# Expert products in three passes: high and low parts written by the first stage's norm, effective weights split as they are made, one buffer for output weights

## The reference, cut to what matters

```
# 1: gradient series + gated feed-forward     x = norm(x + ffn(x) + series(x))
# 2: experts (weights from reference setup: W_org 512x512, 8 pairs of lora_down 512x64
#    and lora_up 64x512, keys, Wq)
q      = mean over tokens of x @ Wq.T
coeff  = softmax(q . keys / sqrt(128))            # 8 numbers for all tokens
w_eff  = W_org.T + sum_e coeff[e] * lora_down[e] @ lora_up[e]
x      = norm(x + x @ w_eff)                       # the expert products
# 3: attention over a single key, which is one product with merged weights
w_val  = sum_g wv[g] @ (sum over 4 heads of wo[g]) # g = 0..7
x      = norm(x + x @ w_val)
# 4: quantised gated feed-forward, and so on
```

## Time and profile before

| what | us |
|---|---|
| three timed executions | 1298.91, 1307.59, 1310.77 |
| their median | 1307.59 |
| the profiled execution, its own time | 1303.14 |
| span of its trace, first to last instruction | 1301.4 |
| PE busy, DVE busy, ACT busy | 1228.7, 719.8, 439.8 |
| DMA queue q1 | 78.32 MB, 16.6% of 16 engines |

### The profile page before, as it was taken

One profiled execution on the slowest core, in us unless ns is written; L12 is line 12 of the kernel. 1 busy time (PEld: TensorE's weight loads), 2 busy tenths in 40 slices (PEclk: granted clock), 3 DMA queues, 4 the chain that ended last, 5 costly groups with the idle time before them and its releaser, 6 DMA issues. The chain is left out here.

```text
span 1301.4 us, 14425 instructions
## 1 busy us (share of the span) xinstructions
PE 1228.7 (94%) x5396; PEld 846.3 (65%) x5396; DVE 719.8 (55%) x1194; ACT 439.8 (34%) x751; POOL 162.2 (12%) x215
## 2 busy tenths in 40 slices
PE   7899999998998999998889999999999988999998
PEld 4788688644876788876565445455455534788886
DVE  4422565576657656453355678677767734443344
ACT  2121422212211114222333223666565566222221
POOL 0000000000086201002112110011011224000000
PEclk9999999999999999998999999999999998999999
DMA  8110023423045561004000010000000001022001
GB/s 346 33 49 16 33 97 131 169 97 146 1 146 194 206 229 26 22 1 138 1 1 1 5 44 1 2 2 1 2 2 2 3 2 49 25 73 73 1 25 41
DMA packets 18265, 79.07 MB, mean 61 GB/s; under 512 B 3104, under 2 KB 3872, under 8 KB 16032
## 3 DMA queue, kind: packets, MB, share of 16 engines
q1 hardware_dynamic: 18208, 78.32, 16.6%
HBM read 75.95 MB, written 2.10 MB: 60 GB/s over the span
## 5 line engine op out<-in xcount | busy, mean ns | idle before, releaser
L2427 DVE TENSOR_REDUCE mqa_top<-psum 128x1 f32<-128x512 f32 (+3 forms) x304 | 186.4, 656 | 50.6 <-PE psum L2219 25.0
L2334 ACT ACTIVATE mqa_prob<-psum 128x512 f32<-128x512 f32 x288 | 156.9, 603 | 85.2 <-PE psum L2249 81.2
L612 PE MATMUL psum<-L_ffn_x,L_ffn_w_up 128*128 128x512 f32 x624 | 143.8, 391 | 8.7 <-DVE L_ffn_hidden L767 7.7
L612 PEld LDWEIGHTS psum<-L_ffn_x,L_ffn_w_up 128*128 128x128 f32 x624 | 116.5, 188 | 36.0 <-DVE L_ffn_hidden L767 10.2
L612 PE MATMUL psum<-L_attn_x,L_attn_w_up 128*128 128x512 f32 x456 | 105.4, 393 | 3.9 <-DVE L_attn_hidden L767 3.9
L612 PEld LDWEIGHTS psum<-L_attn_x,L_attn_w_up 128*128 128x128 f32 x456 | 86.6, 190 | 22.5 <-issue 4.3
L2249 PE MATMUL psum<-mqa_stack_back,mqa_keys 100*128 100x512 f32 x208 | 96.3, 463 | 0.9 <-DVE mqa_stack_front L2418 0.9
L2262 PE MATMUL psum<-mqa_prob,mqa_v 128*32 128x512 f32 x576 | 78.8, 614 | 0.0
L2156 POOL TENSOR_SCALAR_AFFINE_SELECT mqa_prob<-mqa_prob 128x512 f32<-128x512 f32 x64 | 41.7, 671 | 256.6 <-ACT mqa_prob L2334 256.3
L2249 PEld LDWEIGHTS psum<-mqa_stack_back,mqa_keys 100*128 100x128 f32 x208 | 40.0, 192 | 49.6 <-ACT mqa_prob L2334 42.8
L2219 PE MATMUL psum<-mqa_keys,mqa_stack_back 96*128 96x512 f32 (+1 forms) x160 | 67.2, 442 | 4.0 <-ACT mqa_stack_back L2327 1.5
(11 more groups left out here) (301 smaller groups left out, 2060.0 us busy)
## 6 DMA issues: line engine op xcount, KB each, us to landing
L_ffn_stage<-in_L_w SPq DMA_DIRECT2D x25, 768.0 KB, 4.6
L_ffn_z_int<-in_L_z SPq DMA_DIRECT2D x14, 768.0 KB, 4.2
L_ffn_s_all<-in_L_s SPq DMA_DIRECT2D x14, 768.0 KB, 6.0
heads_wo<-in_L_wo SPq DMA_DIRECT2D x8, 1024.0 KB, 4.8
L_attn_stage<-in_L_w SPq DMA_DIRECT2D x10, 512.0 KB, 3.7
L_attn_w_down<-in_L_down SPq DMA_DIRECT2D x1, 2560.0 KB, 24.1
x_feat<-in_x_feat SPq DMA_DIRECT2D x2, 1024.0 KB, 7.0
x_tok<-in_x_tok SPq DMA_DIRECT2D x1, 2048.0 KB, 18.6
```

Source lines behind the costliest of these rows:

```text
L612: ins = nc.tensor.matmul(bank[place][:, :], w_up[:, slot, w_part, at:at + P], x_half[half][:, x_part, k, :], start=k == 0 and n == 0, stop ...
L2334: nc.scalar.activation(prob[:, n % PROBS, :], score_bank[n % 3], ACT.Exp, scale=SCALE)\
L2427: nc.vector.tensor_reduce(top[:, i % 2, 2 if lo == qt * P else lo // HALF, heads[0]:heads[-1] + 1], max_bank[n % 3][:, 0:len(heads) * widt ...
```

## The change

- A class `EntryParts` places low parts of the eight entry tiles in free memory (three under the next front, four from byte 139680, where the second `wo` buffer was, one behind), and `x_high`, a float32r name for the memory of `x_feat`, holds the high parts.
- The first stage's tail gets these parts as its `start`: ACT's copies write the high part, and DVE has one more `dve_low` per tile (tiles 0 to 6 in the first stage's loop, tile 7 in the next block ahead of `c.rot.dve`). The transposes of tile t now wait for the low part of tile t-2 instead of ACT's copy.
- `add_tokens` reads the turn bank in PSUM in place of `x_feat`.
- `MergedHeads.SLOTS` goes from 2 to 1: the load of `wo` g is issued when the sum of g-1 is made.
- `w_values` becomes `w_parts` and serves both stages. After each add of `w_eff` DVE waits for ACT's high copy and subtracts it into the low part, before the next add. PE waits for the four low parts (`eff_low`).
- The expert products go in three passes by the same function as the value products; `product_tiles` stays in use elsewhere.
- The delta product i = 3 waits for the low part of entry tile 7. Steps 10 to 12 stand ahead of the expert products and 13 to 19 behind. `add_heads` 7 moves from tile 2 to tile 4.

The diff, cut to its core (arguments that are only passed through are left out):

```diff
@@ -38,6 +38,8 @@
         self.x_tok = self.sb("x_tok", [P, NT, DIM], F32)
+        with ExitStack() as other_name:
+            self.x_high = self.sb("x_high", [P, KC, TOK], F32R, other_name)
         self.x_feat = self.sb("x_feat", [P, KC, TOK], F32)
@@ -377,6 +379,25 @@
+class EntryParts:
+
+
+    def __init__(self, c, at):
+        with ExitStack() as own:
+            c.sb("entry_below_low", [P, at // 4], F32, own)
+            early = c.sb("entry_low_early", [P, 4, KC, P], F32R, own)
+            c.sb("entry_over_low", [P, 4 * KC * DIM // 2], F32, own)
+            late = c.sb("entry_low_late", [P, KC, P], F32R, own)
+            c.sb("entry_over_late", [P, 8192 // 4 - KC * P], F32, own)
+            first = c.sb("entry_low_first", [P, 3, KC, P], F32R, own)
+        self.high = c.x_high
+        self.low = [first[:, t, :, :] for t in range(3)] + [early[:, t, :, :] for t in range(4)] + [late[:, :, :]]
+        self.x_low = c.sem("entry_x_low")
+
+    def x_part(self, part, t):
+        return self.low[t] if part else self.high[:, :, t * P:(t + 1) * P]
+
+
 class FfnStart:
@@ -476,7 +497,7 @@
         g_bank, u_bank = c.bank[0:2], c.bank[2:4]
-        tail = Tail(c, c.bank[4:6], c.bank[6:8], last is not None)
+        tail = Tail(c, c.bank[4:6], c.bank[6:8], last is not None, start=parts)
@@ -816,11 +837,13 @@
                             expert.add_tokens(dve, tail, earlier)
+                            tail.dve_low(dve, earlier)
                     tail.dve(dve, t)
...
                         expert.add_tokens(dve, tail, t - 2)
+                        tail.dve_low(dve, t - 2)
                     if t + 2 < NT:
@@ -1039,12 +1062,13 @@
         dve.wait_ge(tail.feat_ready, tail.base + t + 1)
-        c.nc.vector.tensor_reduce(c.token_sum[:, :, t], c.x_feat[:, :, t * P:(t + 1) * P], AX.X, ALU.add)
+        turned = tail.tr_bank[t % 2].rearrange("p (k n) -> p k n", k=KC)
+        c.nc.vector.tensor_reduce(c.token_sum[:, :, t], turned, AX.X, ALU.add)
...
-    KV, SLOTS, STEPS = 8, 2, 8 * KC
+    KV, SLOTS, STEPS = 8, 1, 8 * KC
@@ -1052,6 +1076,7 @@
             self.wo = c.sb("heads_wo", [P, self.SLOTS, 4, DIM], F32, own)
+            c.sb("heads_below_wv", [P, 4 * DIM], F32, own)
             self.wv = c.sb("heads_wv", [P, self.KV, DIM], F32, own)
@@ -1121,11 +1146,12 @@
         sb("below_values", [P, 2 * TOK + 4 * KC * P // 2 + 2 * DIM - 256 - KC * DIM])
-        w_values, w_eff = c.sb("lora_w_values", [P, 2, KC, DIM], F32R, own), sb("w_eff", [P, KC, DIM])
+        w_parts, w_eff = c.sb("lora_w_parts", [P, 2, KC, DIM], F32R, own), sb("w_eff", [P, KC, DIM])
         parts = Parts(c, start)
...
         tail_values = Tail(c, c.bank[4:6], c.bank[6:8], start=start)
-        values_ready, values_high = sem("values_ready"), sem("values_high")
+        values_ready, values_high, eff_high = sem("values_ready"), sem("values_high"), sem("eff_high")
+        eff_low = sem("eff_low")
         w_loaded, org_loaded, q_loaded = entry.w_loaded, sem("org_loaded"), entry.q_loaded
@@ -1152,6 +1178,18 @@
             def _(pe):
+                def products(into, x, t):
+
+                    if t >= 2:
+                        pe.wait_ge(into.out_taken, into.base + t - 1)
+                    pe.wait_ge(x.x_low, t + 1)
+                    for k in range(KC):
+                        for n, (x_part, w_part) in enumerate(PASSES):
+                            ins = nc.tensor.matmul(into.out_bank[t % 2], x.x_part(x_part, t)[:, k, :],
+                                                   w_parts[:, w_part, k, :],
+                                                   start=k == 0 and n == 0, stop=k == KC - 1 and n == len(PASSES) - 1)
+                    ins.then_inc(into.out_ready, 1)
+
                 x_last = c.x_tok[:, NT - 1, :]
@@ -1174,7 +1212,7 @@
                     if i == KC - 1:
-                        pe.wait_ge(entry.tail.feat_ready, entry.tail.base + NT)
+                        pe.wait_ge(entry_parts.x_low, NT)
                     for r in range(RC):
@@ -1184,28 +1222,20 @@
                     ins.then_inc(delta_ready, 1)
-                heads.products(pe, range(10, 12))
-                pe.wait_ge(eff_ready, KC)
+                heads.products(pe, range(10, 13))
+                pe.wait_ge(eff_low, KC)
                 for t in range(NT):
-                    product_tiles(c, pe, tail, w_eff, t)
+                    products(tail, entry_parts, t)
                     if t:
...
-                heads.products(pe, range(12, 20))
+                heads.products(pe, range(13, 20))
                 tail.pe(pe, NT - 1)
...
                         pe.wait_ge(values_ready, KC)
-                    if t >= 2:
-                        pe.wait_ge(tail_values.out_taken, tail_values.base + t - 1)
-                    pe.wait_ge(parts.x_low, t + 1)
-                    for k in range(KC):
-                        for n, (x_part, w_part) in enumerate(PASSES):
-                            ins = nc.tensor.matmul(tail_values.out_bank[t % 2], start.x_part(x_part, t)[:, k, :],
-                                                   w_values[:, w_part, k, :],
-                                                   start=k == 0 and n == 0, stop=k == KC - 1 and n == len(PASSES) - 1)
-                    ins.then_inc(tail_values.out_ready, 1)
+                    products(tail_values, parts, t)
                     if t:
@@ -1226,13 +1256,16 @@
                 c.rot.act(act)
+                for i in range(KC):
+                    act.wait_ge(eff_ready, i + 1)
+                    nc.scalar.copy(w_parts[:, 0, i, :], w_eff[:, i, :]).then_inc(eff_high, 1)
                 tail.act(act)
...
                     act.wait_ge(heads.merged, i + 1)
-                    nc.scalar.copy(w_values[:, 0, i, :], c.bank[i]).then_inc(values_high, 1)
+                    nc.scalar.copy(w_parts[:, 0, i, :], c.bank[i]).then_inc(values_high, 1)
                 for t in range(NT):
@@ -1276,18 +1309,22 @@
+                entry.tail.dve_low(dve, NT - 1)
                 c.rot.dve(dve)
...
                         .then_inc(eff_ready, 1)
+                    dve.wait_ge(eff_high, i + 1)
+                    nc.vector.tensor_tensor(w_parts[:, 1, i, :], w_eff[:, i, :], w_parts[:, 0, i, :].bitcast(F32),
+                                            ALU.subtract).then_inc(eff_low, 1)
                 for t in range(NT):
...
                         tail.dve_low(dve, t - 1)
-                    if t in (0, 2):
-                        heads.add_heads(dve, 6 + t // 2)
+                    if t in (0, 4):
+                        heads.add_heads(dve, 6 + t // 4)
                     if start is not None and t == 5:
@@ -1297,7 +1334,7 @@
                     dve.wait_ge(values_high, i + 1)
-                    nc.vector.tensor_tensor(w_values[:, 1, i, :], c.bank[i], w_values[:, 0, i, :].bitcast(F32),
+                    nc.vector.tensor_tensor(w_parts[:, 1, i, :], c.bank[i], w_parts[:, 0, i, :].bitcast(F32),
                                             ALU.subtract).then_inc(values_ready, 1)
@@ -2497,14 +2534,15 @@
         heads = MergedHeads(c, 131488)
-        gradient_ffn(c, a, entry, heads)
+        entry_parts = EntryParts(c, 139680)
+        gradient_ffn(c, a, entry, heads, entry_parts)
         c.rot = Rotation(c)
...
             c.sb("below_lora", [P, 4 * front1.width], F32, scope)
-            lora_then_single_key(c, a, front1, start1, entry, heads)
+            lora_then_single_key(c, a, front1, start1, entry, heads, entry_parts)
         swiglu(c, front1, table=c.rot, ahead=conv_weights, a=a, start=start1)
```

More of the change, by code:

```diff
@@ L444, in swiglu @@
            extra_dve=None, extra_pe=None, extra_act=None, extra_split=None, table=None, ahead=None, a=None,
-           start=None, expert=None, heads=None):
+           start=None, expert=None, heads=None, parts=None):
     nc = c.nc
@@ L890, in products, with gradient_ffn @@
         ins.then_inc(self.used, 1)
-def gradient_ffn(c, a, entry, heads):
+def gradient_ffn(c, a, entry, heads, entry_parts):
     nc = c.nc
@@ L1091, in products, with lora_then_single_key @@
                 ins.then_inc(self.merged, 1)
-def lora_then_single_key(c, a, front, start, entry, heads):
+def lora_then_single_key(c, a, front, start, entry, heads, entry_parts):
     nc = c.nc
```

2 lines of the change are left out of this document (1 added, 1 removed).

## The result

The changed kernel takes 1308.81 us (median of 20 executions, 1302.06 to 1314.39), the kernel before in the same comparison 1305.48 (20 executions, 1296.99 to 1310.77). The ratio is 1.0046 with a 95% interval of 1.0027 to 1.0064: slower by some 6 us, by 3.5 at the least, so within 1%. The forecast was 1312.1. The profiled execution of the kernel after took 1312.02 us, that of before 1303.14.

The account below looks back on a forecast made before the run. The prediction took DVE to pace the expert products, with PE waiting for it, and PE to be the path behind. Its terms, 6.46 - 0.54 - 0.34 - 0.86 + 2.0 = 6.7 us, on 1305.4 gave 1312.1 us, range 1302 to 1321.

Parts of the forecast that it names:

- part 4: From tile 0's add to tile 7's transposes: 5.92 us late, less 0.34 and 0.86, so PE 4.7 us late, nothing recovered behind.
- What bounds the kernel: In the expert products DVE sets the pace once tile 0's product is there, and PE waits; behind them PE is the path.
- Part 1: Expert products: three passes save PE 4.5 us, but only 0.54 and 0.34 reach DVE, 0.9 us at the end.
- Part 2: Entry tile 7's low part ahead of the rotation chain: chain and first `w_eff` add 1.8 us later, bounds 1.3 and 1.9.
- Part 3: Split of `w_eff`: serial rounds of 2.09 us, first expert product 6.46 us later, PE waiting 5.4 (3.4 to 6.2).
- Part 5: Low clock behind PE's wait ahead of the expert products: 2.0 us lost, bounds 0 and 2.8.
- Part 6: First-stage low parts, token sum read from PSUM, and loads with one `wo` buffer: all covered, costed at nothing.
- Rival (a): Same PE wait ahead of the expert products, but clock at full: +4.7 us, 1310.1; chance 0.18.
- (b): Loads behind the single `wo` buffer land late and DVE stands at `dequantise`: 5 us on top, 1317; chance 0.10.
- (c): Split hides behind heads' steps, shorter products carry through: 4.5 us off, 1300.9; gain if PE waits under 1.7; chance 0.07.
- (d): Three passes no faster on the expert products' operands: the 0.9 us returns, 1313; chance 0.03.

Follow-up runs that it names:

- heads_ahead: Changed kernel with six more steps of heads ahead of the expert products and fewer behind: 1309.36 us, ratio 1.0045.
- steps_in_stretch: Changed kernel with seven steps of heads moved into PE's waits inside the expert products: 1308.14 us, ratio 1.0050.
- plain_products: Changed kernel with the expert products as plain float32 of the entry's high part and `w_eff`, splits and waits kept: 1304.90 us, ratio 1.0038.
- low_part_in_chain: Changed kernel with entry tile 7's low part inside the rotation chain, where DVE waits for ACT's root, instead of ahead of it: 1310.28 us, ratio 1.0062.
- split_in_a_row: Changed kernel with DVE's four adds of `w_eff` in a row and the four subtractions behind them: 1306.01 us, ratio 1.0017.
- turns_on_pool: Changed kernel with the nine levels of turn factors computed by GpSimd instead of in DVE's chain: 1300.35 us, ratio 0.9981.
- best_with_plain_products: filled_turns_on_pool with plain float32 expert products of the entry's high part and `w_eff`, low part left out: 1298.86 us, ratio 0.9995.
- filled_turns_on_pool: filled plus turn factors on GpSimd, heads sum 6 ahead of the `w_eff` split, next front's second low part behind the value-weight split: 1294.95 us, ratio 0.9943.
- filled: Changed kernel with `w_eff` subtractions one add behind, entry tile 7's low part inside the chain, heads steps inside the stretch: 1303.04 us, ratio 0.9992.
- 14 memsets: Changed kernel with fourteen more GpSimd memsets in the setup, starting everything some 3.4 us later: 1314.86 us, ratio 1.0087.

## Why the prediction was right

It said slower by 6.7 us; the ratio gives 6.0 (3.5 to 8.4), and the two medians of 20 differ by 3.3. The level that it took for the kernel before, 1305.4, is the median of the 20 executions, 1305.48, and that is luck: in the three later comparisons the same kernel stood at 1301.6 to 1302.4. The mechanism is the forecast one, a wait of PE for a split that DVE reaches late. But the size is closer than the sum deserves: in the profile the first value product is 7.8 us later, with one term of the sum wrong by 1.7 us (part 4), and others that partly make up for it. Step by step:

- **What bounds the kernel.** Held. DVE paced the stretch: from tile 0's add to tile 6's no idle time, 26.15 us (26.56 before). It is 26.16 in heads_ahead and 26.15 in steps_in_stretch, whatever PE does there, and 27.20 in plain_products, where the longer products behind tile 0's cost DVE 1.05.
- **Part 1** (0.54 and 0.34 us): -0.41 us in place of -0.34 inside the stretch. The 0.54 shows where the clock is up: 3.10 us from start to add in low_part_in_chain, against 3.64 before.
- **Part 2** (1.8 us): the first add of `w_eff` stands 0.27 us ahead of the first heads row in place of 1.97, so 1.7 later. Taking it away gave 1.46.
- **Part 3** (a round 2.09, PE 6.46 late after a wait of 5.4): 1.98, 6.06 and 5.03. Of the three hand-overs that I had put at 0.04 each, the two between DVE and ACT are 0.03 (264.03 - 264.00, 264.68 - 264.65), and the next add starts 0.08 before the subtraction's row ends. split_in_a_row and turns_on_pool show that this wait comes from the place of the rounds in DVE's order.
- **Part 4** (PE 4.7 us late at the transposes of tile 7): this is the mis-sized term. I gave 0.86 us back for fourteen rows instead of sixteen; between tile 6's add and the first value product 0.84 us were lost instead. The difference, 1.7 us, is the second low clock. Its root stands in part 1, "the rest only lets PE wait longer for DVE", which I costed at nothing. PE's waits for DVE inside the stretch grew from 2.2 to 6.1 us in total, and the clock fell behind the last one. That they are the cause is shown by plain_products and steps_in_stretch, both with shorter waits and no second fall. All thirteen profiles agree: the seven kernels with 6.0 to 6.1 us of these waits have the low clock behind the stretch, and the six with 2.9 us or less have none (before has 2.2). Whether the sum of the waits counts or the longest of them (3.3 us against 2.7 at the most) is not told apart.
- **Part 5** (2.0 us of clock at the head): tile 0's add came 4.97 us after the product's start, 3.10 at full clock: 1.87.
- **Part 6** (nothing): held. The first stage's low part is done before the transposes, which wait no longer than before (6 rounds alike):

```profile
195.73 0.69 DVE L1066 TENSOR_REDUCE token_sum<-psum 128x4 f32<-128x512 f32 x1
...
196.33 0.68 DVE L133 TENSOR_TENSOR entry_low_first<-psum,x_high 128x512 fp32r<-128x512 f32 x1
...
197.83 0.60 PE L155 MATMUL psum<-ident,x_tok 128*128 128x128 f32 x4
```

The sum read from PSUM takes 0.69 us against 0.68. And the loads stand behind tile 0 and its sum of g = 6 at 281, as said, with `dequantise` 18 us later and no wait in brackets:

```profile
280.95 0.33 SPq L1090 DMA_DIRECT2D heads_wo<-in_L_wo  x1
281.32 0.43 SPq L229 DMA_DIRECT2D L_ffn_stage<-in_L_w  x1
...
298.94 1.75 DVE L352 TENSOR_TENSOR L_ffn_stage<-L_ffn_stage,L_ffn_z_int 128x1536 f32<-128x1536 int32 x1
```

- **Rival (a)**, the clock at full: not in the profile, where both lows are seen. **(b)**, late loads: no. **(c)**, the products carry through: not here; with PE's gaps filled they do, for 4.7 us, where it named 4.5. The break-even that (c) names, a wait of 1.7 us, is too high. It leaves out the extra step of heads in front: in turns_on_pool, with no wait, the first expert product starts 0.61 us later than before. And it leaves out the second low clock, by which the first value product is 1.64 us later there. **(d)**, three passes no faster: no, as part 1 shows.

The profile moved by 7.8 us at the first value product, and the time by 6.0, with an interval of 3.5 to 8.4 that holds both. The executions differ in their mean granted clock, and at a like clock the kernels stand nearly in the order of the profiles. At 0.989 to 0.990: before 1298.8 (8 executions of the later comparisons), after 1302.3 (3), plain_products 1304.2 (6), split_in_a_row 1299.5 (4), turns_on_pool 1298.7 (4), best_with_plain_products 1298.0 (6), filled_turns_on_pool 1292.4 (4). This leaves the change 3.4 us. At 0.987 to 0.988 it is 4.7 (before 1302.1, 27 executions; after 1306.8, 7), and at 0.980 it is 3.8 (1308.5, 3; 1312.2, 6). (The executions of the changed kernel are from the first comparison.) All three are near the 4.7 of the sum without its clock term. But this picks executions by a number that the change itself moves, so I read it as a hint.

For low_part_in_chain, steps_in_stretch and filled the first value product is 3 to 11 us earlier than in the changed kernel, and the ratios of the first two show none of it. For steps_in_stretch and filled a part of it (2.6 and 2.4 us) is given back at the low clock of the value products, and that is seen in the profiles: filling PE's gaps made the next wait longer, and the clock fell behind that one. The remainder lies further on. No execution of low_part_in_chain or filled was above a mean clock of 0.985, and none of steps_in_stretch above 0.983, while the kernel before reaches 0.993. Why the later code gets less clock in these kernels is not shown.

## What to carry to other kernels

When a split is put between a sum and its consumer, look first at what stands ahead of it in that engine's order: here a chain of small operations that nobody waited for held four rounds of add, copy and subtract, and moving the chain was worth 6.2 us at the first value product, against 3.4 for adds and subtractions in a row behind it. Shorter products pay only where their engine sets the pace: the same three passes were worth 0.3 us with PE waiting for DVE, and 4.7 us once PE had other work in its gaps. And "it only waits longer" is a cost: price the waits that an edit adds inside a stretch that another engine paces, by what the clock does behind them.

## What the hardware showed that I had not expected

- One wait's length did not tell whether the clock falls. Behind 1.95 us (split_in_a_row) tile 0's add came 4.65 us after the product's start, behind 3.57 us (low_part_in_chain) 3.10, which is full speed, and behind 5.03 it came at 4.97. At the value products a wait of 2.07 us had a low clock behind it in best_with_plain_products (4.65 us to the add) and none in filled_turns_on_pool (3.09). My bound between 3.11 and 3.90 was none.
- The same code, from the first value product to the end (in the last two versions with one tile's split moved into it), took 975 to 992 us in thirteen profiles, and behind 330 us the low clock took between 6.85 and 27.2 us of full speed. It is the largest unsteady thing in this kernel, larger than all that the change does. These are single executions: in four of the twelve changed kernels the profiled one was the slowest of all its executions, and with 14 memsets it was the fastest. Which of the small gaps cost clock in an execution, and which don't, stays open.
- Forty-five GpSimd operations of 128x4 beside the other engines cost nothing that the profile shows: its busy time went from 162.4 to 174.6 us.

```profile
span 1291.7 us, 14511 instructions
PE 1220.4 (94%) x5417; PEld 850.4 (66%) x5428; DVE 721.6 (56%) x1169; ACT 442.1 (34%) x755; POOL 174.6 (14%) x261
```

This is the page of filled_turns_on_pool. PE is busy 10.2 us less than in the changed kernel with the same products. Most of that is clock and not work; eleven of its rows are missing from this trace (5417 against 5428 weight loads), which is worth a few us.
